# Joining the products of v and of the state, with a buffer of masked scores and decayed q for each chunk of a block

## What is computed

```python
x  = L0_attn_x                      # (4, 1024, 1024)
xn = layernorm(x)
qkv = rmsnorm(xn) @ ternary(qkv_w).T          # 16 heads of 64
# per sequence, chunks of 128 tokens, per head:
#   scores = q k^T * mask              mask[t, s] = exp(-decay (t - s)) for t >= s, else 0
#   o      = scores v + (q * lam_t) S  lam_t = exp(-decay t)
#   S      = lam_T S + (k * lam_rev)^T v
s   = rmsnorm(rmsnorm(o)) @ ternary(proj_w).T
g   = silu(xn @ ternary(ffn_w).T + bias)
out = x + s * g
```

## Time and profile before

| | |
|---|---|
| median of 3 runs | 1314.8 us (1313.32 to 1315.18) |
| span of the profiled execution | 1314.2 us |
| PE busy | 1289.1 us, 98% |
| DVE busy | 1008.4 us, 77% |
| ACT busy | 617.4 us, 47% |
| POOL busy | 600.4 us, 46% |
| HBM traffic over the span | 67 GB/s |

### The profile page before, as it was taken

The page is one execution under the profiler, slowest core; times in us unless marked ns, Lnnn a source line. Parts: engine busy times, 40 slices in busy tenths (PEclk is TensorE's granted clock), DMA queues, the critical chain, the costliest instruction groups (busy, mean ns, idle before and its releaser), DMA issues.

```text
span 1314.2 us, 25908 instructions
## 1 busy us (share of the span) xinstructions
PE 1289.1 (98%) x10263; PEld 824.8 (63%) x10263; DVE 1008.4 (77%) x1567; ACT 617.4 (47%) x1216; POOL 600.4 (46%) x537
## 2 busy tenths in 40 slices
PE   4999999999999999999999999999999999999998
PEld 2577767675665757566574656657566575756655
DVE  7888367687676887878788787877878788787755
ACT  5884144344434635446354544644436363544621
POOL 1442785955354435354432535435333443535352
PEclk9999999999999999999999999999999999999999
DMA  9631101203012030210303011030300304021020
GB/s 361 248 97 66 57 34 37 101 33 106 1 38 100 17 121 18 76 46 18 121 17 120 18 57 65 17 121 18 94 28 19 119 17 121 17 58 49 1 65 32
DMA packets 33433, 90.32 MB, mean 69 GB/s; under 512 B 10529, under 2 KB 10785, under 8 KB 33314
## 3 DMA queue, kind: packets, MB, share of 16 engines
q1 hardware_dynamic: 33024, 88.65, 20.0%
q10 hardware_dynamic: 290, 0.02, 0.0%
HBM read 71.85 MB, written 16.81 MB: 67 GB/s over the span
## 4 chain that ended last, share of the span: by engine, by line
PE 94%; DVE 2%; ACT 2%; DMA 1%; issue 1%; SPq 0%; POOL 0%; DVEq 0%; ACTq 0%; POOLq 0%
PE ring L854 20%; PE ring L787 13%; PE ring L813 13%; PE ring L839 12%; PE ring L1012 10%; PE ring L988 5%; PE att_ps L892 4%; PE att_ps L942 4%; PE att_ps L938 4%; PE ring L904 2%; PE att_ps L919 2%; PE ring L867 1%; PE ring L754 1%; DMA raw<-in_ffn_w 1%; ACT junk L1951 1%
## 5 line engine op out<-in xcount | busy, mean ns | idle before, releaser
L854 PE MATMUL ring<-b_lo,qkv_q 128*128 128x256 f16 x1216 | 268.2, 272 | 0.0
L854 PE MATMUL ring<-b_hi,qkv_q 128*128 128x256 f16 x1216 | 268.2, 273 | 0.0
L2532 POOL TENSOR_TENSOR xt<-xt,gate_even 128x512 f32<-128x512 f32 x58 | 90.6, 1564 | 172.5 <-DVE gate_even L1626 131.8
L854 PEld LDWEIGHTS ring<-b_hi,qkv_q 128*128 128x128 fp8e4 x1216 | 120.2, 99 | 15.8 <-issue 0.4
L854 PEld LDWEIGHTS ring<-b_lo,qkv_q 128*128 128x128 fp8e4 x1216 | 118.9, 98 | 15.6
L2506 POOL TENSOR_TENSOR sq<-sq,cols 128x1024 f32<-128x1024 f32 x29 | 55.0, 1896 | 126.8 <-DVE b_lo L1423 118.6
L2094 ACT ACTIVATE gate_even<-gate_even 128x512 f32<-128x512 f32 x60 | 37.3, 625 | 136.2 <-DVE gate_even L1454 136.1
L942 PE MATMUL att_ps<-arena 128*64 128x128 f32 x1024 | 95.0, 273 | 0.0
L938 PE MATMUL att_ps<-arena 128*64 128x128 f32 x896 | 88.5, 276 | 0.0
L1523 DVE TENSOR_TENSOR arena<-att_ps,mask 128x512 f32<-128x512 f32 x128 | 79.3, 680 | 11.0 <-PE att_ps L892 11.0
L2385 POOL TENSOR_TENSOR ln<-ln,small 128x3 f32<-128x3 f32 x32 | 37.4, 1168 | 100.2 <-DVE ln L1311 99.3
(11 more groups left out here) (298 smaller groups left out, 3523.1 us busy)
## 6 DMA issues: line engine op xcount, KB each, us to landing
xt<-in_x SPq DMA_DIRECT2D x60, 512.0 KB, 3.7
out<-xt SPq DMA_DIRECT2D x31, 512.0 KB, 2.7
raw<-in_qkv_w SPq DMA_DIRECT2D x24, 512.0 KB, 15.8
y<-in_x_turned SPq DMA_DIRECT2D x14, 512.0 KB, 5.9
y_odd<-in_x_turned SPq DMA_DIRECT2D x14, 512.0 KB, 6.7
raw<-in_ffn_w SPq DMA_DIRECT2D x8, 512.0 KB, 9.8
norm_rows<-norm_out SPq DMA_DIRECT2D x14, 256.0 KB, 6.0
raw<-in_proj_w SPq DMA_DIRECT2D x6, 512.0 KB, 4.7
```

Source lines behind the costliest of these rows:

```text
L854: ins = pe.matmul(ring[:, b, e * BT:(e + 1) * BT], qkv_q[:, cb, o:o + P], part[:, cb, :], start=(cb == 0 and part is b_hi and (e == 0 or i ...
L2532: pool.tensor_tensor(o, o, gate_of(i)[:, c, cs], ALU.add).then_inc(s_add, 1)
```

## The change

- v and the state lie in one tile: `v_state` has, for each head, 64 rows of v's first 64 tokens above 64 rows of the state. The state moves from both halves of the partitions to the upper half for all heads. v's rows are brought there by a DMA of 64 x 4 KB on ACT's queue (`copy_v`), one for each chunk that isn't first.
- Masked scores and decayed q lie in one tile too, `stacks[c]`, one for each chunk of a block, in three slots of 64 columns a head: slot 0 masked scores of the first 64 columns (rows 0 to 63, all that isn't zero by the mask) above decayed q of these tokens; slot 1 masked scores of the last 64 columns on all 128 rows; slot 2 zeros above decayed q of the last 64 tokens. The joined product takes slots 0 and 2, 128 columns; a second one takes v by slot 1, 64 columns. A first chunk takes v by slots 0 and 1.
- `decay_q` writes both parts of q, for the even heads from partitions 0 to 63 to 64 to 127: two instructions of 64x1024 a chunk, in the place of two of 128x512, each followed by a wait for its own end. Chunk 1's comes before the attention, behind the additions to the output; only in block 0 does it stay where it was.
- `decay_state` is one instruction of 64x1024. The zeros of slot 2 are set once.
- Waits follow: masking waits for the outputs of the same chunk of the block before; outputs wait for both q instructions and for v's copy; where the tiles lie over others, waits for the last users are added. The scratch memory of the DMA descriptors is cut to 2048.

```diff
-        QL_OFF = V_OFF + CHUNKS * C
-        ST_OFF = QL_OFF + 2 * C
+        KD_OFF = V_OFF + CHUNKS * C
+        ST_OFF = KD_OFF + C
         SM_OFF = ST_OFF + 2 * PR * P
-        ARENA = SM_OFF + H * T
+        ARENA = SM_OFF + H * 3 * D
...
-        with nc.sbuf_tensor("arena", [P, ARENA], F32) as arena:
-            pass
-        sb("arena_low", [P, SM_OFF])
-        o_row = sb("o_row", [P, CPH, T])
-        o_split = sb("o_parts", [P, 3, 2, CPH, T], F16)
+        arena = sb("arena", [P, ARENA])
...
-        v_tok = arena[:, V_OFF:QL_OFF].rearrange("p (c n) -> p c n", c=CHUNKS)
-        q_decay = arena[:, QL_OFF:QL_OFF + C].rearrange("p (r t) -> p r t", r=PR)
-        k_decay = arena[:, QL_OFF + C:QL_OFF + 2 * C]
+        v_tok = arena[:, V_OFF:KD_OFF].rearrange("p (c n) -> p c n", c=CHUNKS)
+        k_decay = arena[:, KD_OFF:KD_OFF + C]
         ow_first = k_decay.rearrange("p (r t) -> p r t", r=PR)
-        state = arena[:, ST_OFF:SM_OFF].rearrange("p (k r e) -> p k r e", k=2, r=PR)
-        scores_m = arena[:, SM_OFF:ARENA].rearrange("p (h e r t) -> p h e r t", h=HALF, e=2, r=CPH)
-        b_turned = arena[:, SM_OFF:ARENA].rearrange("p (c j t) -> p c j t", c=CHUNKS, j=NCB)
+        v_state = arena[:, ST_OFF:SM_OFF].rearrange("p (k r e d) -> p k r e d", k=2, r=PR, e=2)
+        stack_even = arena[:, SM_OFF:ARENA].rearrange("p (s e r t) -> p s e r t", s=3, e=2, r=PR)
...
+        with nc.sbuf_tensor("b_turned", [P, CHUNKS, NCB, T], F32) as b_turned:
+            pass
+        with nc.sbuf_tensor("stack_odd", [P, 3, 2, PR, D], F32) as stack_odd:
+            pass
+        o_row = sb("o_row", [P, CPH, T])
+        o_split = sb("o_parts", [P, 3, 2, CPH, T], F16)
+        sb("stack_odd_last", [P, 2, PR, D])
+        stacks = stack_even, stack_odd
...
+        def decays(g):
+            return sum(not is_first(k) and not is_last(k) for k in range(g + 1))
...
+        def copied(i, c):
+            return DMA * sum(not is_first(chunk(k, c)) for k in range(i + 1))
+        def joined(g):
+            return v_state[:, passes_on(g) % 2, :, :, :]
...
             def outputs(i, c, half):
                 g = chunk(i, c)
                 n = HALF * g + half
-                if not is_first(g):
-                    pe.wait_ge(s_ql, HALF * takes_over(g) + half + 1)
-                    if half == 0:
-                        pe.wait_ge(s_st, 2 * passes_on(g))
+                if not is_first(g) and half == 0:
+                    pe.wait_ge(s_ql, 2 * takes_over(g) + 2)
+                    pe.wait_ge(s_st, 2 * passes_on(g))
+                    pe.wait_ge(s_vcopy[c], copied(i, c))
+                    if takes_over(g) == 0:
+                        pe.wait_ge(s_zeros, CHUNKS)
                 if half == 0:
                     for by in v_at(i, c):
                         pe.wait_ge(*by)
                 pe.wait_ge(s_scm, 2 * (n + 1))
                 for j in range(CPH):
                     r = half * CPH + j
-                    if not is_first(g):
+                    to = [att_ps[e * D:(e + 1) * D, half, j, :].rearrange("p (s t) -> p s t", s=2) for e in range(2)]
+                    v = [v_tok[:, c, r * P + e * D:r * P + (e + 1) * D] for e in range(2)]
+                    if is_first(g):
                         for e in range(2):
-                            pe.matmul(att_ps[e * D:(e + 1) * D, half, j, :],
-                                      state[:, passes_on(g) % 2, r, e * D:(e + 1) * D], q_decay[:, r, :],
-                                      start=True, stop=False, skip_group_check=True)
+                            ins = pe.matmul(to[e], v[e], stacks[c][:, 0:2, e, r, :], start=True, stop=True)
+                        continue
                     for e in range(2):
-                        ins = pe.matmul(att_ps[e * D:(e + 1) * D, half, j, :],
-                                        v_tok[:, c, r * P + e * D:r * P + (e + 1) * D],
-                                        scores_m[:, half, e, j, :], start=is_first(g), stop=True,
-                                        skip_group_check=True)
+                        pe.matmul(to[e], joined(g)[:, r, e, :], stacks[c][:, 0:3:2, e, r, :],
+                                  start=True, stop=False, skip_group_check=True)
+                    for e in range(2):
+                        ins = pe.matmul(to[e][:, 1, :], v[e], stacks[c][:, 1, e, r, :],
+                                        start=False, stop=True, skip_group_check=True)
                 ins.then_inc(s_o, 1)
...
-                if c == 0 and i > 0 and by_products(i - 1):
+                if c == 1 and i > 0 and by_products(i - 1):
                     dve.wait_ge(s_ops, of_o_product(i - 1, "p3"))
+                early = slice(0, P if is_first(g) else D)
                 for half in range(HALF):
+                    hs = slice(half * CPH, (half + 1) * CPH)
                     dve.wait_ge(s_sc, HALF * g + half + 1)
-                    if g > 0:
-                        dve.wait_ge(s_o, HALF * (g - 1) + half + 1)
-                    for e in range(2):
-                        dve.tensor_tensor(scores_m[:, half, e, :, :], att_ps[:, 2 * half + e, :, :],
-                                          mask[:, e, half * CPH:(half + 1) * CPH, :], ALU.mult).then_inc(s_scm, 1)
+                    if i > 0:
+                        dve.wait_ge(s_o, of_half(i - 1, c, half))
+                    for s, rows in enumerate((early, slice(0, P))):
+                        ts = slice(s * D, (s + 1) * D)
+                        dve.tensor_tensor(stacks[c][rows, s, :, hs, :], att_ps[rows, 2 * half:2 * half + 2, :, ts],
+                                          mask[rows, :, hs, ts], ALU.mult).then_inc(s_scm, 1)
...
-                    dve.wait_ge(s_state0, 1)
+                    dve.wait_ge(s_wout, w_n["qkv", QKV_TILES - 1])
                 if is_first(g):
                     if g > 0:
                         dve.wait_ge(s_o, HALF * g)
                 else:
-                    dve.wait_ge(s_sd, 2 * (passes_on(g) - (g // NCHUNK + 1)) + 2)
+                    dve.wait_ge(s_sd, decays(g))
                 for e in range(2):
-                    rows, cs = slice(e * D, (e + 1) * D), slice(e * D, (e + 1) * D)
-                    to = state[rows, (n + 1) % 2, :, cs]
+                    rows = slice(e * D, (e + 1) * D)
+                    to = v_state[D:P, (n + 1) % 2, :, e, :]
                     if is_first(g):
                         dve.tensor_copy(to, kv_ps[rows, :, :]).then_inc(s_st, 1)
...
+            def copy_v(i, c):
+                g = chunk(i, c)
+                if is_first(g):
+                    return
+                for by in v_at(i, c):
+                    act.wait_ge(*by)
+                if g > 1:
+                    act.wait_ge(s_o, HALF * (g - 1))
+                else:
+                    act.wait_ge(s_wout, w_n["qkv", QKV_TILES - 1])
+                act.dma_start(joined(g)[0:D, :, :, :].rearrange("p r e d -> p (r e d)"),
+                              v_tok[0:D, c, :]).then_inc(s_vcopy[c], DMA)
...
             def attention_by_tokens(i, c):
                 if c == 0:
                     take_v(i, 1)
+                    copy_v(i, 1)
                     base_z(i)
                     turned_k(i, 1)
                     if i + 1 < NB:
...
             for i in range(BY_TOKENS, NB):
@@ -2369,6 +2413,7 @@
                 if i + 1 < NB:
                     high_b(i + 1, 0, 0)
                     high_b(i + 1, 0, 1)
+                copy_v(i, 0)
                 attention_by_tokens(i, 0)
                 attention_by_tokens(i, 1)
...
-            def decay_q(i, c, half):
+            def decay_q(i, c):
                 g = chunk(i, c)
                 if is_first(g):
                     return
-                n = takes_over(g)
-                hs = slice(half * CPH, (half + 1) * CPH)
-                pool.wait_ge(s_q, CPH * i + 2 * (half + 1))
-                if n == 0 and half == 0:
+                pool.wait_ge(s_q, CPH * (i + 1))
+                if takes_over(g) == 0:
                     pool.wait_ge(s_tables, TABLES)
-                if n > 0:
-                    pool.wait_ge(s_o, HALF * (g - 1) + half + 1)
-                pool.tensor_tensor(q_decay[:, hs, :], q_t[:, hs, c * T:(c + 1) * T], lam_q[:, hs, :],
-                                   ALU.mult).then_inc(s_ql, 1)
+                if i > 0:
+                    pool.wait_ge(s_o, of_half(i - 1, c, 1))
+                if c == 1 and i > 1:
+                    pool.wait_ge(s_bslo, of_b_sum(i, "S4"))
+                if c == 1 and i > 0 and by_products(i - 1):
+                    pool.wait_ge(s_ops, of_o_product(i - 1, "p3"))
+                    pool.wait_ge(s_add, of_out(i - 1, 0, 1))
+                elif c == 1 and is_first(g - 1):
+                    pool.wait_ge(*((s_zeros, 2) if i == 0 else (s_pwsum, 3)))
+                elif c == 0 and i + 1 == NB:
+                    pool.wait_ge(s_gamma, chunk(i - 1, 1) + 1)
```

(40 more changed lines are left out.)

15 lines of the change are left out of this document (11 added, 4 removed).

## The result

The changed kernel takes 1364.1 us (median of 4 runs, 1362.8 to 1364.5) against 1314.9 before: ratio 1.0377, 95% interval 1.0363 to 1.0392. The direction was forecast, the size not: 1349 was given, and 1364.1 lies 1.1 us above the range. The profiled execution has a span of 1362.8 us, 48.6 more than before.

A forecast was written before the change was run, and what follows sets the result against it. PE was taken to bound the kernel, busy 1289.1 of 1314.2 us. 58.0 us of new waits against 23.6 gained made +34.4 on 1314.8: 1349 us, forecast range 1336 to 1363, wider range 1301 to 1363.

The forecast's parts named there:

- PE's part: Outputs of the 28 chunks not first in a sequence: one 128-column and one 64-column product per head, 23.6 us less.
- POOL's durations: Decaying q takes 2.35 us per 64x1024 instruction, two a chunk; decaying the state becomes one of 1.90 us.
- Rival 1: POOL's instructions are cheap, 1.90 us instead of 2.35: 1328 us (1320 to 1336), chance 0.20.
- The waits: New PE waits because DVE is held by POOL's longer or moved instructions: 58.0 us in all.
- Collision 1: Chunk 0's longer q beside DVE's centring delays L1407 (now L1427); PE waits 1.7 us in 8 blocks: 13.6 us.
- Collision 2: Chunk 1's moved q holds DVE's decay of k's tokens; PE waits 2.9 us more in 8 blocks: 23.2 us.
- Blocks 8 and 12: Blocks beginning a sequence, with no POOL work there before: the decay of k's tokens ends later, 6.2 us of waits.
- Block 3: Start-up block: POOL's longer instructions alternate with DVE's centring, so v's sums end later and PE waits 6.8 us.
- Block 15: Last block, no centring: 1.1 us of waits at the first place and 0.8 at the second, 1.9 us.
- Block 1: Start-up block: POOL is busy without a break until L2525 (now L2588), for which PE waits 5.4 us.
- The step that failed: Reading of the kernel before: PE at full clock in practically every slice, so 2.4 GHz and no gain from the clock.
- Rival 4's second half: Chunk 0's copy of v lands after 6.0 us, 1 us late in 12 blocks: 1361 to 1375; whole rival's chance 0.07.

The follow-up runs named there:

- a3_scores_twice: The changed kernel with PE computing the scores of chunk 0 twice in blocks 4 to 15: 1354.5 us, ratio 1.0288.
- h7_and_block_1: h4_q0_between_additions with chunk 0's copy of v cut in two and, in block 1, the sum of weights T3 behind output scale, state decay and L1620: 1307.0 us.
- h4_q0_between_additions: The changed kernel with chunk 0's q between first and second output additions, chunk 1's q and block 3's both behind the decay of k: 1318.2 us.
- a4_q_by_one_operand: The changed kernel with POOL's two q instructions multiplying by the constant 0.5 instead of the table, leaving out q's decay: 1305.7 us, ratio 0.9917.
- a1_q1_in_the_middle: The changed kernel with chunk 1's q decayed in the middle of the attention again, behind the bias additions: 1358.4 us, ratio 1.0317.
- c1_only_chunk1_behind_k: The changed kernel with chunk 1's q decayed only after DVE's decay of k's tokens of chunk 0, from block 4 on: 1324.2 us, ratio 1.0051.
- h5_and_block_1: h4_q0_between_additions with block 1's output scale and state decay ahead of the sum of weights T3: 1318.0 us, ratio 1.0009.

## Why the prediction failed where it did

**PE's part, right.** 23.6 us were given, 22.7 came; a 64-column record does pass in 28 ns behind one of 128. The Trainium skill (TensorE: Matmul & The Clock Gate, section LDWEIGHTS) has a load take columns / 1.2 ns, by estimate 53 ns for 64 columns. Read as a lower bound of a step, that would have made the gain nothing; the trace doesn't bear that reading out, as each of these records has a load of its own.

**POOL's durations, right.** Undisturbed, a 64x1024 takes 2.34 us (2.35 taken), and the state 1.90. Rival 1, with 1.90 for q, is out.

**The waits, right in place and 8 us too large in sum**, 58.0 against 50.2:

- Collision 1 (q of chunk 0): 13.6 given, 9.3 measured. The two DVE instructions that meet it took 2.83 and 2.62 us, 1.9 us more than the pair of the earlier trace rows took; the slack of 0.5 read between L1407's end and PE's start was nearer to 0.75, so 1.17 us were left of 1.7.
- Collision 2 (q of chunk 1): 23.2 given, 8 x 2.53 = 20.2 measured, as L1555's pair grew by 2.6 and not 2.9. Blocks 8 and 12: 6.2 given, 5.9. Block 3: 6.8 given, 5.9. Block 15: 1.9 given, 0.6.
- Block 1: 5.4 given, a wait of 5.6 on L2588 came. Block 0's 1.9 us was not given.

**The step that failed is the first one**, "the level is 2.4 GHz and nothing is to be had from it". True of the kernel before, it was then carried into a kernel with a wait of 2.5 to 6 us in twelve blocks (1, 3 and 5 to 14). The sum added the waits and left out that PE runs at 1.2 GHz after them: 18.0 us, and 3.2 for the restarts, against none given. +34.4 as forecast, less 7.8 for the waits, plus 18.0, 3.2 and 0.9 (the outputs' smaller gain) is +48.7. No rival held this either; the upper end of 1363 was the forecast's own spread, and two errors of 8 and 21 us with opposite signs left the time 1.1 us above it, so that it came so near is luck. That the filled waits of a3_scores_twice kept the level shows the cause, and h7_and_block_1, which has no wait over 2.0 us behind the start-up and no stretch at half clock, agrees.

**Rival 4's second half was right as a mechanism and wrong in its place.** The copy of v "lands after 6.0 us like the broadcast": in the changed kernel it lands after 2.8 to 4.2 us and nobody waits. In h4_q0_between_additions, with the collisions gone, it lands up to 6.7 us after its issue and costs 8.0 us. It is not that the collisions had only hidden this: in a4_q_by_one_operand both are gone too, and PE waits without a named releaser at the outputs just once in blocks 5 to 14, 0.8 us, there too with a load issued 0.3 us ahead of the copy. What differs is which load stands beside the copy and how early the copy is issued (in block 9 6.8 us ahead of the outputs in the changed kernel, 5.1 us ahead of their due time in h4_q0_between_additions), and both move with the order of the lists.

**What the prediction said it would see**, it saw: half of the outputs' records of 64 columns, L828 on L1419 with 2 to 3 us (2.53, in blocks 8 and 12 2.94), the product on k_sum_last on L1427, the wait on L2588; q's instructions at 2.34 undisturbed and L1555 at 2.8 each. Not seen was PE's busy time 23 us less, and that one line gave the clock away.

Open is why two waits of the same 2.5 us, in blocks 10 and 14, were followed by no stretch at half clock, and four of eleven of 2.2 to 2.5 us in a1_q1_in_the_middle neither. The eight waits of 1.17 us never were, those of 5.6 and 5.9 were both times. The wait of 1.9 us in block 0, which nearly every kernel here has, was followed by one of 3.41 us in c1_only_chunk1_behind_k and in h5_and_block_1, and not in the changed kernel. So a wait of about 2 us may cost clock or not, and one profile doesn't settle it. No run was made to part the cases.

## What to carry to other kernels

A wait that a change gives TensorE is to be priced twice, once for its length and once for what the engine computes slowly behind it; here 50 us of waits brought 18 us more. When an edit makes a GpSimd instruction with two SBUF operands longer or moves it, look which VectorE instruction with two SBUF operands starts beside it: the hold is the whole instruction, so its length counts, and either a cut (43 us here for no work saved) or a place beside work from PSUM takes it away. And when the first late engine is mended, expect the next one close behind: here the sum of squares, 1.5 us late, then a DMA that had seemed hidden, once the new order had put it beside a load. After such a move read the landing times of the DMAs again.
